# A perceiver block on one NeuronCore: gate and up weights as high and low fp32r parts, the first state as mask and add, and a shorter route

## The reference, cut to what matters

```python
# x (128 x 256) attends to ctx (12544 x 256), x1 = x + attention
# h0 = layernorm(x1); then a gated delta rule block with 8 heads:
q, k, v = split(silu(causal_dwconv(x @ W_qkvz, conv_w)))      # conv of 4 taps
# per step t: S = exp(g_t) S; delta = (v_t - k_t S) beta_t; S += k_t delta^T; o_t = q_t S
core = rmsnorm(o) * silu(z);  h = h0 + core @ W_out
x2 = rmsnorm(h)
probs = softmax(x2 @ W_router); topv, topi = top_k(probs, 2)
route = sum(one_hot(topi) * topv / sum(topv))
moe = sum_e route_e * ((silu(x2 @ W_gate_e) * (x2 @ W_up_e)) @ W_down_e)   # 8 experts of 128
# x3 = layernorm(x1 + h + moe); a second layer of 8 experts (256 -> 1024 -> 256) with top 2 follows
```

## Time and profile before

| | |
|---|---|
| median of 3 runs | 231.6 us (231.24 to 232.49) |
| profiled execution | 233.11 us |
| its span, first to last instruction | 231.3 us |
| busy PE, DVE, ACT, POOL | 220.9, 143.0, 142.3, 124.1 us |
| granted clock of TensorE | 1.00 of full speed throughout |

### The profile page before, as it was taken

The page is one execution under the profiler, slowest core; times in us unless marked ns, Lnnn a source line. Parts: engine busy times, 40 slices in busy tenths (PEclk is TensorE's granted clock), DMA queues, the critical chain, the costliest instruction groups (busy, mean ns, idle before and its releaser), DMA issues.

```text
span 231.3 us, 4173 instructions
## 1 busy us (share of the span) xinstructions
PE 220.9 (96%) x1547; PEld 193.1 (83%) x1547; DVE 143.0 (62%) x343; ACT 142.3 (62%) x259; POOL 124.1 (54%) x82
## 2 busy tenths in 40 slices
PE   8999979999999999889989999989999999999994
PEld 7757858888888887779879999864789999999993
DVE  2246646666666667536995776434343759887783
ACT  5157677777777775636776555555316847777570
POOL 1139858889998888730799930300000544555550
PEclk9999999999999999999999999999999999999999
DMA  6999999999999704999980000000000686960000
GB/s 187 368 425 421 411 418 420 419 413 419 417 418 417 310 8 143 418 422 422 412 364 9 1 3 0 3 0 0 1 3 0 195 347 231 414 268 1 3 0 23
DMA packets 8532, 52.94 MB, mean 229 GB/s; under 512 B 953, under 2 KB 1218, under 8 KB 6466
## 3 DMA queue, kind: packets, MB, share of 16 engines
q1 hardware_dynamic: 8514, 52.69, 56.8%
HBM read 52.56 MB, written 0.13 MB: 228 GB/s over the span
## 4 chain that ended last, share of the span: by engine, by line
PE 74%; DVE 10%; DMA 7%; ACT 4%; issue 2%; POOL 2%; ACTq 1%; DVEq 0%; POOLq 0%
PE psum L474 26%; PE psum L554 11%; PE psum L808 8%; DMA late_sb<-in_ctx_T 7%; PE psum L469 6%; PE psum L530 5%; PE psum L465 3%; PE psum L688 3%; PE psum L701 3%; DVE work L1237 2%; POOL ctx_lo L382 2%; PE psum L731 2%; PE psum L572 1%; DVE ring L1304 1%; PE psum L759 1%
## 5 line engine op out<-in xcount | busy, mean ns | idle before, releaser
L382 POOL TENSOR_TENSOR ctx_lo<-ring,ctx_hi 128x1792 fp32r<-128x1792 f32 x13 | 52.6, 4045 | 14.1 <-ACT ctx_hi L874 14.1
L457 POOL TENSOR_TENSOR h_lo<-ring,h_hi 128x512 fp32r<-128x512 f32 x16 | 24.7, 1546 | 54.5 <-ACT h_hi L1072 48.4
L474 PE MATMUL psum<-late_sb,work 128*128 128x448 f32 x68 | 27.9, 542 | 0.7 <-DMA late_sb<-in_ctx_T 0.7
L474 PE MATMUL psum<-xT,late_sb 128*128 128x128 f32 x224 | 26.4, 276 | 0.1
L474 PEld LDWEIGHTS psum<-xT,late_sb 128*128 128x128 f32 x224 | 25.6, 192 | 0.3 <-DVE xT L1418 0.3
L881 ACT ACTIVATE probsT_hi<-psum 128x512 fp32r<-128x512 f32 (+1 forms) x28 | 13.7, 541 | 19.4 <-PE psum L469 18.1
L874 ACT ACTIVATE ctx_hi<-ring 128x1792 fp32r<-128x1792 f32 x13 | 22.1, 1701 | 3.5 <-DMA ring<-in_ctx 3.5
L1132 DVE TENSOR_REDUCE smalls<-psum 128x1 f32<-128x896 f32 x14 | 15.3, 1092 | 14.3 <-PE psum L530 9.1
L1156 DVE TENSOR_TENSOR probsT_lo<-psum,probsT_hi 128x512 fp32r<-128x512 f32 (+1 forms) x28 | 16.2, 619 | 8.5 <-ACT probsT_hi L881 8.4
L474 PEld LDWEIGHTS psum<-late_sb,work 128*128 128x128 f32 x68 | 11.9, 190 | 9.1 <-issue 8.7
L469 PE MATMUL psum<-early_sb,work 128*128 128x128 f32 x122 | 17.1, 274 | 0.2 <-ACT work L1026 0.2
(11 more groups left out here) (265 smaller groups left out, 492.4 us busy)
## 6 DMA issues: line engine op xcount, KB each, us to landing
late_sb<-in_ctx_T SPq DMA_DIRECT2D x14, 896.0 KB, 14.0
ring<-in_ctx SPq DMA_DIRECT2D x14, 896.0 KB, 13.2
late_sb<-in_late SPq DMA_DIRECT2D x10, 825.0 KB, 10.8
late_sb<-in_experts SPq DMA_DIRECT2D x8, 1024.0 KB, 10.3
late_slots<-in_experts SPq DMA_DIRECT2D x8, 1024.0 KB, 12.3
early_sb<-in_early SPq DMA_DIRECT2D x1, 512.0 KB, 3.8
early_sb<-in_early SPq DMA_DIRECT2D x1, 465.0 KB, 17.9
work<-in_levels SPq DMA_DIRECT2D x1, 416.0 KB, 20.2
```

What stands on the lines that cost most here:

```text
L382: nc.gpsimd.tensor_tensor(ctxNv[1][:, r % 2], ring[:, r], ctxNv[0][:, r % 2], ALU.subtract).then_inc(s["ctx_lo"], 1)
L457: nc.gpsimd.tensor_tensor(hT[1][:, e % 2, at, :], h32[:, at, :], hT[0][:, e % 2, at, :], ALU.subtract).then_inc(s["h_lo_done"], 1)
L474: last = nc.tensor.matmul(o, lhs(c), rhs(c), start=(c == 0), stop=(c == n - 1))
```

## The change

The gate and up weights are split into high and low fp32r parts: the high parts are copied by ScalarE in four pieces, the low parts subtracted by GpSimd, two pieces ahead of the power function and two behind it. They lie in memory of `late_slots`, so the third and fourth expert are fetched only after the last gate/up product. The transposed x2 gets parts too. Each of the four gate/up groups becomes six one-pass products. The first state is the masked product plus the identity. The route is worked out from the sum and the difference of the two masks, which are already halved and scaled, and the sum for `xh` moves behind it. A spare SiLU is put ahead of the Tanh. The key product comes behind three of the queries' first taps, not four. The router's logits go to another bank. Three pairs of semaphores are merged (`ln_sd` for `sd1_done`, `ln_xn` for `xz_done` and `xf_done`).

```diff
+            GU = parts(overlay, "gate_up", 2 * DC * E * P)      # same memory as late_slots
...
+        gate_up_parts = [part[:, :].rearrange("p (w c b n) -> p w c b n", w=2, c=DC, b=2) for part in GU]
+        x2_parts = [part[:, 0:D] for part in (h_hi, h_lo)]
+        GATE_UP = ((0, 0), (1, 0), (0, 1), (1, 1))
...
@@ SyncE
                 if j == W_SLOTS:
-                    sp.wait_ge(s["pv_done"], NG)
+                    sp.wait_ge(s["gu_mm"], 4)
...
@@ GpSimd, behind convolve_v(1)
+            def gate_up_lo(i):
+                w, b = GATE_UP[i]
+                pool.wait_ge(s["gu_hi"], i + 1)
+                nc.gpsimd.tensor_tensor(gate_up_parts[1][:, w, :, b, :], gate_up_32[:, w, :, b, :], gate_up_parts[0][:, w, :, b, :],
+                                        ALU.subtract).then_inc(s["gu_lo"], 1)
+            gate_up_lo(0)
+            gate_up_lo(1)
             for b in range(2):
                 pool.wait_ge(s["ms_done"], b + 1)
                 nc.gpsimd.tensor_tensor(s_("f", 4 * b, 4 * b + 4), s_("ms", 4 * b, 4 * b + 4), ..., ALU.pow)
+            gate_up_lo(2)
+            gate_up_lo(3)
...
@@ TensorE
-            wide(bank[1][:, D:D + E], lambda c: half(xT, c), lambda c: w_router[:, c, :]).then_inc(s["lg_mm"], 1)
-            def gate_up(b, o, w):
-                wide(bank[o + b][:, :], lambda c: half(xT, c), lambda c: w[:, c, 512 * b:512 * (b + 1)]).then_inc(s["gu_mm"], 1)
+            wide(bank[7][:, 0:E], lambda c: half(xT, c), lambda c: w_router[:, c, :]).then_inc(s["lg_mm"], 1)
+            pe.wait_ge(s["x2_hi"], 2)
+            def gate_up(i):
+                w, b = GATE_UP[i]
+                pe.wait_ge(s["gu_hi"], i + 1)
+                terms = [(u, v, c) for u, v in ((0, 0), (0, 1), (1, 0)) for c in range(DC)]
+                for t, (u, v, c) in enumerate(terms):
+                    if t == DC:
+                        pe.wait_ge(s["gu_lo"], i + 1)
+                    if t == 2 * DC:
+                        pe.wait_ge(s["x2_lo"], 2)
+                    last = nc.tensor.matmul(bank[3 + 2 * w + b][:, :], half(x2_parts[u], c), gate_up_parts[v][:, w, c, b, :],
+                                            start=(t == 0), stop=(t == len(terms) - 1))
+                last.then_inc(s["gu_mm"], 1)
...
-            gate_up(0, 3, w_gate)
-            gate_up(0, 5, w_up)
-            gate_up(1, 3, w_gate)
+            gate_up(0)
+            gate_up(1)
+            gate_up(2)
             products(0)
-            gate_up(1, 5, w_up)
+            gate_up(3)
...
@@ ScalarE
+            def gate_up_hi(i):
+                nc.scalar.activation(gate_up_parts[0][:, w, :, b, :], gate_up_32[:, w, :, b, :], ACT.Copy).then_inc(s["gu_hi"], 1)
...
             silu_v(1)
             silu_z(0)
+            gate_up_hi(0)
             copy_xt(6)
             keep_columns(6)
+            gate_up_hi(1)
...
                 nc.scalar.activation(coreT[:, 4 * b:4 * b + 4, :], ...)
+                if b == 0:
+                    gate_up_hi(2)
             nc.scalar.activation(s_("spare", 0, 1), s_("eps", 3, 4), ACT.Sqrt).then_inc(s["act_chain"], 1)
             chain[0] += 1
+            gate_up_hi(3)
...
             nc.scalar.activation(half(xT, 1), bank[2][:, 0:P], ACT.Copy, scale=s_("w2p", 1, 2)).then_inc(s["x2_copied"], 1)
+            nc.scalar.activation(half(x2_parts[0], 1), bank[2][:, 0:P], ACT.Copy, scale=s_("w2p", 1, 2)).then_inc(s["x2_hi"], 1)
             link(nc.scalar.activation(scratch[:, :], hh[:, :], ACT.Square, accum_out=s_("sd", 0, 1)))
             nc.scalar.activation(s_("sd", 1, 2), s_("sd", 0, 1), ACT.Sqrt, scale=1.0 / D, bias=s_("eps", 2, 3)).then_inc(s["hsd_done"], 1)
+            nc.scalar.activation(s_("spare", 0, 1), s_("eps", 3, 4), ACT.Silu).then_inc(s["act_chain"], 1)
...
@@ VectorE
-            taps(1, (1,))
+            for k in range(3):
+                tap(1, 1, k).then_inc(s["dve_chain"], 1)
             dve.wait_ge(s["tanh_kb"], 2)
             dve.wait_ge(s["conv_done"], 1)
             V.scalar_tensor_tensor(k, ..., 1.0, k, ALU.add, ALU.mult).then_inc(s["k_done"], 1)
+            tap(1, 1, 3).then_inc(s["dve_chain"], 1)
...
-                V.copy_predicated(x0, mask.bitcast(U32), a).then_inc(s["x_done"], 1)
+                link(V.tensor_tensor(a, a, mask, ALU.mult))
+                V.tensor_tensor(x0, a, x0, ALU.add).then_inc(s["x_done"], 1)
...
+            V.tensor_scalar(half(x2_parts[0], 0), bank[1][:, 0:P], s_("w2p", 0, 1), None, ALU.mult).then_inc(s["x2_hi"], 1)
+            dve.wait_ge(s["x2_hi"], 2)
+            for c in range(DC):
+                V.scalar_tensor_tensor(half(x2_parts[1], c), bank[1 + c][:, 0:P], s_("w2p", c, c + 1), half(x2_parts[0], c),
+                                       ALU.mult, ALU.subtract).then_inc(s["x2_lo"], 1)
             dve.wait_ge(s["hsd_done"], 1)
             V.reciprocal(s_("rs", 0, 1), s_("sd", 1, 2)).then_inc(s["x2_done"], 1)
-            link(V.tensor_tensor(xh[:, :], x1[:, :], hh[:, :], ALU.add))
+            link(V.tensor_scalar(s_("w", 0, 1), s_("rs", 0, 1), 0.5, None, ALU.mult))
...
-                link(V.tensor_scalar(s_("e1"), early_at("iota"), s_("idf", 0, 1), None, ALU.is_equal))
-                link(V.tensor_scalar(s_("e2"), early_at("iota"), s_("idf", 1, 2), None, ALU.is_equal))
+                V.tensor_scalar(s_("e1"), early_at("iota"), s_("idf", 0, 1), weight, ALU.is_equal, ALU.mult).then_inc(s["dve_chain"], 1)
+                V.tensor_scalar(s_("e2"), early_at("iota"), s_("idf", 1, 2), weight, ALU.is_equal, ALU.mult).then_inc(s["dve_chain"], 1)
...
+                V.tensor_tensor(s_("lg"), s_("e1"), s_("e2"), ALU.subtract).then_inc(s["dve_chain"], 1)
+                V.tensor_tensor(s_("top"), s_("e1"), s_("e2"), ALU.add).then_inc(s["dve_chain"], 1)
...
                 dve.wait_ge(s["tanh_done"], turn)
-                link(V.tensor_scalar(s_("w", 0, 1), s_("th"), 0.5, 0.5, ALU.mult, ALU.add))
-                link(V.tensor_scalar(s_("w", 1, 2), s_("th"), -0.5, 0.5, ALU.mult, ALU.add))
-                link(V.tensor_scalar(s_("e1"), s_("e1"), s_("w", 0, 1), None, ALU.mult))
-                return V.scalar_tensor_tensor(out, s_("e2"), s_("w", 1, 2), s_("e1"), ALU.mult, ALU.add)
+                return V.scalar_tensor_tensor(out, s_("lg"), s_("th"), s_("top"), ALU.mult, ALU.add)
...
-            link(V.tensor_scalar(s_("route"), s_("route"), s_("rs", 0, 1), None, ALU.mult))
+            link(V.tensor_tensor(xh[:, :], x1[:, :], hh[:, :], ALU.add))
```

More of the change, by code:

```diff
@@ L98, in perceiver @@
             ctxN = parts(overlay, "ctx", 2 * GT * D)
+        with ExitStack() as overlay:
+            GU = parts(overlay, "gate_up", 2 * DC * E * P)
+        assert 4 * DC * E * P <= (SLOTS - W_SLOTS) * EXPERT_N
         late_slots = sb("late_slots", (SLOTS - W_SLOTS) * EXPERT_N)
@@ L135, in perceiver @@
         w_out = late_at("out", c=HV)
-        w_gate = late_at("gate", c=DC)
-        w_up = late_at("up", c=DC)
         w_down = late_at("down", c=E)
+        gate_up_32 = W_sb[:, LATE["gate"][0]:LATE["up"][1]].rearrange("p (w c b n) -> p w c b n", w=2, c=DC, b=2)
+        gate_up_parts = [part[:, :].rearrange("p (w c b n) -> p w c b n", w=2, c=DC, b=2) for part in GU]
+        x2_parts = [part[:, 0:D] for part in (h_hi, h_lo)]
         w_router = late_at("router", c=DC)
@@ L214, in perceiver @@
             an_T x_done t_mm t_done xt_T xt_done xx_mm zt_mm za_done zb_done o_mm osq_done ms_done f_done core_dve core_act zo_done raw_v core_T coreT_done
-            out_mm h_done hsd_done x2_done x2_T x2_copied lg_mm dm_in tanh_done gu_mm gact_done prod_done prod_T prodT_done
-            moe_mm xf_done xf_T xf_copied r1_mm rel_dve rel_act sc_mm gate_done gate_T gateT_done b2_mm
+            out_mm h_done hsd_done x2_done x2_T x2_copied x2_hi x2_lo gu_hi gu_lo lg_mm dm_in tanh_done gu_mm gact_done prod_done prod_T prodT_done
+            moe_mm xf_T xf_copied r1_mm rel_dve rel_act sc_mm gate_done gate_T gateT_done b2_mm
             h_mm w2_hi_done w2_lo_done h_act h_dve h_hi_done h_lo_done y_mm h0_done b2_added""".split()
@@ L918, in _ @@
             act.wait_ge(s["var_done"], 2)
-            nc.scalar.activation(s_("sd", 1, 2), s_("mv", 1, 2), ACT.Sqrt, bias=s_("eps", 1, 2), scale=1.0 + RMS_EPS).then_inc(s["sd1_done"], 1)
-            nc.scalar.activation(s_("sd", 0, 1), s_("mv", 1, 2), ACT.Sqrt, bias=s_("eps", 0, 1)).then_inc(s["sd1_done"], 1)
+            nc.scalar.activation(s_("sd", 1, 2), s_("mv", 1, 2), ACT.Sqrt, bias=s_("eps", 1, 2), scale=1.0 + RMS_EPS).then_inc(s["ln_sd"], 1)
+            nc.scalar.activation(s_("sd", 0, 1), s_("mv", 1, 2), ACT.Sqrt, bias=s_("eps", 0, 1)).then_inc(s["ln_sd"], 1)
             act.wait_ge(s["xz_T"], 1)
@@ L1035, in _ @@
             nc.scalar.activation(half(xT, 1), bank[2][:, 0:P], ACT.Copy, scale=s_("w2p", 1, 2)).then_inc(s["x2_copied"], 1)
+            nc.scalar.activation(half(x2_parts[0], 1), bank[2][:, 0:P], ACT.Copy, scale=s_("w2p", 1, 2)).then_inc(s["x2_hi"], 1)
```

(11 more changed lines are left out.)

28 lines of the change are left out of this document (18 added, 10 removed).

## The result

The changed kernel takes 230.19 us (median of 6 runs, 229.77 to 230.52), the kernel before 231.42 us (6 runs, 231.10 to 232.49); ratio 0.9912, 95% interval 0.9883 to 0.9941. In a second comparison it was 230.26 against 232.03, ratio 0.9932 (0.9907 to 0.9957). The ratios are estimates of their own and not the quotients of the medians, which are 0.9947 and 0.9924. Every execution on record counts as undisturbed, so that does not explain the difference, and the first quotient lies outside the interval of its ratio; what the two have in common is the direction. The change is faster, by 0.9 and 0.7% by the ratios and by 0.5 and 0.8% by the medians, where I forecast 0.56%. Its size is better read from the trace.

What follows compares the result with a forecast made beforehand. TensorE held 74% of the chain, but keep-warm products hid which edit pays; VectorE ran without a stop from 113 to 121.6 us. Terms -0.45 + 0.15 - 1.0 = -1.3 us gave 230.3 against 231.6; range 229.5 to 232.3.

Steps and rivals of the forecast that it cites:

- First state: VectorE, 119.09 to 121.63: masked product and stepped sum per half take about 2.1 us instead of 2.54, -0.45 us.
- Rival 2: First state on VectorE: stepped access, not the predicate, was the cost; +0.9 in place of -0.45, total 231.6; chance 0.10.
- High copy ahead of level 6: ScalarE: first 1.04 us copy in a gap of 0.99, which shrinks by some 0.1 more; +0.15 us (0 to 0.4).
- Subtractions on GpSimd: GpSimd: two 2.39 us subtractions end at 143 before the power at 144.62, two run later, hidden; 0.
- Rival 3: ScalarE's first copy and GpSimd's two subtractions push level 6 and the power by 0.4 each; -0.7 in all, 230.9; chance 0.12.
- Experts: Attention block's experts: cheaper gate/up groups, shorter route and one table load fewer bring the second products sooner; -1.0 us (0.7 to 1.3).
- Behind the second products: After the second four gated products of the attention block's experts, everything is as before; 0.
- Later fetch of two experts: Transfers wait for the last gate/up group, about 161, and end at 171, first wanted at 182.69; 0.
- Key product: VectorE near 113.39: product trades places with a 0.28 us tap, VectorE still sets the time; 0, within 0.05.
- Rival 1: ScalarE in the experts: Tanh not in SiLU's tables, spare SiLU costs a load; +0.7 in all, 232.3; chance 0.16.

Runs made afterwards that it cites:

- first state only: The kernel before with only the predicated copy of the first state replaced by the masked product and the sum; ratio to the kernel before 0.9958 (0.9938 to 0.9978).

## Why the prediction was right or wrong, point by point

- **Direction and mechanisms: right.** Faster, through the first state and the experts, with the key product and the later fetch worth nothing. **The sum: too small**, 1.3 us forecast, 1.66 in the trace, 2.0 and 1.6 by the two ratios (0.0088 and 0.0068 of 231.4), 1.2 and 1.8 by the medians. 0.56% lay just outside the first interval (0.59% to 1.17%), inside the second (0.43% to 0.93%). The median of 230.19 lay within the range.
- **First state, -0.45:** measured -0.48 (Z, in the variant with it alone too). The product took 0.43 and the stepped sum 0.63; 0.43 and 0.61 were read from the earlier trace rows. Rival 2 is refuted: with steps of 128 columns the sum costs what the reordering sums of the levels cost. By elimination the time of the old copy lay in the predicated operation itself; one without steps was not tried.
- **High copy ahead of level 6, +0.15: this step failed.** It cost 0.00: Z is at 38.22 with it and without it (first state only). I set the copy's busy time, 1.04, against the idle time of 0.99. The gap itself I had put too large, if anything: with the first state alone changed it is 0.83, behind the same wait for GpSimd (0.15; 0.18 in the changed kernel). But instructions of ScalarE that follow each other overlap, here at both ends of the copy. It started at 134.97, 0.47 behind the start of an activation of 0.58 (134.50), and its successor at 135.92, 0.95 after it. The two together need 0.47 + 0.95 = 1.42 from start to start. With the first state alone the neighbours stood 1.41 apart:

```profile
134.23 0.58 ACT L974 ACTIVATE work<-psum 128x512 f32<-128x512 f32 x1
135.64 0.39 ACT L980 ACTIVATE ring<-psum 128x256 f32<-128x256 f32 x1 [0.83 <-PE psum L469]
```

Level 6's first copy came at 34.97 after x1 instead of 34.93, and by Z the 0.04 were gone. (The Trainium skill, ScalarE: Activation LUTs, section What ACT_TABLE_LOAD costs, says that activations in a row overlap by about 93 ns. By that, with an overlap at each end, a copy of 1.04 would need a gap of about 0.85, an estimate, where I counted on 0.89. The trace agrees: 1.05 busy, 0.95 from start to start.)
- **Subtractions on GpSimd, 0:** right. 2.38 and 2.35, 2.39 read; cover 1.48 us, 1 us forecast. Rival 3 is refuted on both its legs.
- **Experts, -1.0:** measured -1.04 from h to the second products. With 1.80 us added, by which h is earlier in the changed profile (150.49 against 152.29), the first activation stood at 156.17 (forecast 156.4), the end of the route at 157.18 (157.05), the first products at 157.67 (157.5), their transposes at 158.85 (158.85), the second products at 160.99 (161.0). The six matmuls took 1.37, not 1.45. Each small miss was on one side of a wait and lost in it. One reading was off: the router's part ends near 154.4 by the earlier trace rows (159.59 less twelve times 0.43), not 154.3, and the first group stood at 154.20 (152.40 + 1.80); nothing hung on it.
- **What the -1.0 is made of: not said clearly enough.** The prediction followed the events and so had the sum right, but it gave no sign that the two halves are worth 0.06 and 0.18 alone. The experiments showed that.
- **Behind the second products, 0:** measured -0.13 to -0.14, missing from the sum. It is a stall of the kernel before whose cause is open, so this part of the gain is luck. The sign was in the earlier trace rows, where the same four instructions take 1.12 at 158.37 and 1.26 at 162.03, and I read over it; that the change would lose it, no row of before could say.
- **Later fetch of two experts, 0:** right. Their transfers started at 159.12 and filled two slices of 5.7 us; nothing behind them moved, from O to the last sum of the kernel it is 61.99 us before (166.72 to 228.71) and 61.98 after (163.75 to 225.73).
- **Key product, 0:** right, and shown by undoing it.
- **Rival 1 (Tanh not in SiLU's tables), +0.7:** refuted by the rows of ScalarE. The spare SiLU decides 0.8 us, so the 0.16 that I gave it was a bet on what no row of before could show, and that it was won is in part luck.

The terms, then: -0.48, 0.00, -1.04, -0.14 make -1.66 where I had -0.45, +0.15, -1.0, 0. Of the missing 0.36, 0.15 is the copy ahead of level 6, 0.14 the stall on VectorE, and 0.07 the two main terms.

## What to carry to other kernels

Follow the events of each engine through the stretch that an edit touches, and find which wait ends last after the edit; here two changes worth 0.06 and 0.18 us alone (the cheaper products; the shorter route with its spare SiLU) were worth 1.04 together, because each removed the wait behind which the other was hidden. Count an inserted instruction and the gap from start to start (0.47 + 0.95 against 1.41), not busy time against idle time (1.04 against 0.83). Two executions of one kernel can differ by a microsecond ahead of the stretch that was changed, so measure a small change from an event in front of it to one behind it: there repeats agreed within 0.02 us, where the ratio of the runs was known to 0.6. And before a difference of 0.1 to 0.2 us is put down to an edit, look whether the instructions next to it still take what they took: a stall of 0.14 came and went here with edits elsewhere.

## What the runs showed of the hardware that I had not expected

A predicated copy of 256 columns costs 1.27 us apiece in a pair, a product and a stepped sum of the same columns 0.43 and 0.63. And four VectorE instructions with no wait between them took 1.26 or 1.12 us according to whether two empty instructions stood some 160 us ahead of them. With the stream on VectorE left alone and one instruction taken from ScalarE, four of the same kind took 1.25 instead of 1.12. Another variant had 0.23 us ahead of them for which no wait is named; whether that is the same is open. What makes these stalls, the profile does not show.
